# A windowed-attention block on one core: VectorE adds bias and residual in all eight tiles instead of six

## The reference

```python
xn = _ln2d(x, norm1_g, norm1_b)
xn = jnp.roll(xn, shift=(-SHIFT, -SHIFT), axis=(2, 3))
windows = _window_partition(xn, win)
attn_out = _mha(windows, in_w, in_b, out_w, out_b)
attn_out = attn_out @ proj_w.T + proj_b
y = _window_reverse(attn_out, win, hp, wp, b)
y = jnp.roll(y, shift=(SHIFT, SHIFT), axis=(2, 3))
y = shortcut + y                                # the step that the change is about
z = _ln2d(y, norm2_g, norm2_b)
z = jnp.einsum('bchw,oc->bohw', z, fc1_w) + fc1_b[None, :, None, None]
z = jax.nn.gelu(z, approximate=False)
z = jnp.einsum('bchw,oc->bohw', z, fc2_w) + fc2_b[None, :, None, None]
return y + z
```

## Time and profile before

| what | value |
|---|---|
| median of 3 runs | 91.69 us (91.31 to 93.89) |
| profiled execution, its own time | 91.67 us |
| its span, first to last instruction | 89.9 us |
| mean granted TensorE clock | 0.979 of full |
| PE busy | 80.4 us (89%) |
| DVE busy | 65.1 us (72%) |
| POOL busy | 53.3 us (59%) |
| ACT busy | 50.8 us (56%) |

### The profile page before, as it was taken

The page is one execution under the profiler, slowest core; times in us unless marked ns, Lnnn a source line. Parts: engine busy times, 40 slices in busy tenths (PEclk is TensorE's granted clock), DMA queues, the critical chain, the costliest instruction groups (busy, mean ns, idle before and its releaser), DMA issues.

```text
span 89.9 us, 4248 instructions
## 1 busy us (share of the span) xinstructions
PE 80.4 (89%) x1770; PEld 47.4 (53%) x1770; DVE 65.1 (72%) x208; ACT 50.8 (56%) x85; POOL 53.3 (59%) x64
## 2 busy tenths in 40 slices
PE   5987999888999998999997958949999999999960
PEld 5975756545774666647645525525464444243420
DVE  4999989989899799799788895992470763333060
ACT  0494998980579287485763615623449496353500
POOL 7978829982866917996954878579305225800000
PEclk9999999999999999999999999998599999999999
DMA  1899300110111111111021110000000000030233
GB/s 28 217 368 423 157 22 7 55 63 32 44 37 44 51 47 37 65 40 55 30 66 37 51 50 30 0 7 0 7 0 7 0 0 0 7 117 24 93 138 99
DMA packets 3619, 5.74 MB, mean 64 GB/s; under 512 B 1072, under 2 KB 1840, under 8 KB 3472
## 3 DMA queue, kind: packets, MB, share of 16 engines
q1 hardware_dynamic: 2736, 3.08, 10.3%
q10 hardware_dynamic: 864, 2.39, 7.1%
HBM read 2.65 MB, written 1.05 MB: 41 GB/s over the span
## 4 chain that ended last, share of the span: by engine, by line
PE 49%; POOL 19%; DVE 16%; issue 11%; ACT 1%; POOLq 0%; DVEq 0%
POOL max_x L1045 9%; PE ps_s L320 7%; PE ps_u L484 5%; PE ps_u L411 4%; PE ps_s L468 4%; POOL rstd L1054 3%; DVE stats L624 3%; PE ps_t L468 3%; POOL rstd_x L1061 3%; PE ps_t L320 3%; DVE row_max L644 3%; PE ps_m L468 2%; PE ps_o L437 2%; PE ps_o L425 2%; PE ps_o L484 2%
## 5 line engine op out<-in xcount | busy, mean ns | idle before, releaser
L1045 POOL TENSOR_TENSOR max_x<-max_t,early 128x512 bf16<-128x512 bf16 x14 | 14.7, 1049 | 11.3 <-DVE max_t L657 11.3
L644 DVE TENSOR_REDUCE row_max<-ps_s 128x16 f32<-128x1024 f32 x15 | 18.2, 1213 | 2.7 <-PE ps_s L320 2.4
L914 ACT ACTIVATE probs<-ps_t 128x1024 f32<-128x1024 f32 x13 | 13.3, 1025 | 10.2 <-PE ps_t L394 9.8
L320 PE MATMUL ps_s<-masked,qk 32*64 32x256 f32 x240 | 16.4, 386 | 1.9 <-DMA masked<-qk 0.8
L320 PE MATMUL ps_t<-masked,qk 32*64 32x256 f32 x224 | 15.3, 387 | 0.0
L1054 POOL TENSOR_TENSOR rstd<-y_var,minus_half 128x4 f32<-128x4 f32 x8 | 8.3, 1034 | 8.8 <-DVE y_var L703 8.7
L320 PEld LDWEIGHTS ps_s<-masked,qk 32*64 32x64 f32 x240 | 8.2, 131 | 5.6 <-DVE row_max L644 1.8
L411 PE MATMUL ps_u<-probs,vz 128*32 128x64 f32 x512 | 10.9, 228 | 0.0
L411 PEld LDWEIGHTS ps_u<-probs,vz 128*32 128x32 f32 x512 | 8.2, 113 | 3.6 <-issue 3.2
L1030 POOL TENSOR_TENSOR rstd<-var,minus_half 128x4 f32<-128x4 f32 x8 | 8.5, 1060 | 1.0 <-DVE var L632 0.4
L663 DVE STREAM_TRANSPOSE sums<-ps_u 128x512 f32<-128x512 f32 x8 | 5.7, 707 | 4.0 <-PE ps_u L411 4.0
(11 more groups left out here) (115 smaller groups left out, 154.9 us busy)
## 6 DMA issues: line engine op xcount, KB each, us to landing
masked<-qk SPq DMA_DIRECT2D x54, 32.0 KB, 1.9
x_ch<-x_ch_d ACTq DMA_DIRECT2D x1, 1024.0 KB, 8.3
out_d<-result SPq DMA_DIRECT2D x3, 256.0 KB, 2.5
x_tok<-x_tok_d ACTq DMA_DIRECT2D x1, 512.0 KB, 6.3
late<-late_d ACTq DMA_DIRECT2D x1, 352.0 KB, 4.6
x_tok<-x_tok_d SPq DMA_DIRECT2D x2, 128.0 KB, 3.4
x_tok<-x_tok_d ACTq DMA_DIRECT2D x1, 256.0 KB, 4.3
out_d<-result SPq DMA_DIRECT2D x2, 128.0 KB, 2.3
```

Of the source, the lines that this page charges most:

```text
L320: return nc.tensor.matmul(ps[o:o + L, g, n * TOK:(n + 1) * TOK], qk[r:r + RG, b, w, t], masked[r:r + RG, b, :, w, t], start=(n == 0), stop ...
L644: nc.vector.tensor_reduce(row_max[:, w, 0:16], score_bank(k, w)[:].rearrange("q g (h j) -> q (g h) j", j=L), axis=AX.X, op=ALU.max).then_i ...
L914: nc.scalar.activation(probs[:, w, :], scores_t_bank(k, w)[:].rearrange("q g c -> q (g c)"), ACT.Exp).then_inc(probs_done, 1)
L1045: nc.gpsimd.tensor_tensor(max_x[:, k % 2, w, :].rearrange("q (n i) -> q n i", n=16), bf16_high(max_t[:, w, :]).unsqueeze(1).to_broadcast([ ...
```

## The change

The set `SPLIT` is emptied, and what served it is taken out: the tile `y_part`, its semaphore, `bias_y` on ACT and `residual` on POOL. DVE's `residual` is called for all eight tiles.

```diff
-        y_part = sb("y_part", [P, TOK])
...
-        SPLIT = (TILES - 5, TILES - 4)
...
-                if tile_ok(t - 2) and t - 2 not in SPLIT:
+                if tile_ok(t - 2):
                     residual(t - 2)
...
-            def bias_y(k):
-                act.wait_ge(out_projected, k + 1)
-                if k > SPLIT[0]:
-                    act.wait_ge(y_done, k)
-                nc.scalar.activation(y_part[:], ps_o[:, 0, 0:TOK], ACT.Identity, bias=b_out[:, 0:1]).then_inc(y_part_done, 1)
...
-                if t - 2 in SPLIT:
-                    bias_y(t - 2)
...
-            def residual(k):
-                pool.wait_ge(y_part_done, k - SPLIT[0] + 1)
-                nc.gpsimd.tensor_tensor(y_all[:, tokens(k)], y_part[:], x_ch[:, tokens(k)], op=ALU.add).then_inc(y_done, 1)
...
-                if t - 2 in SPLIT:
-                    residual(t - 2)
```

More of the change, by code:

```diff
@@ L186, in swin_block_kernel @@
         out_projected = sem("out_projected")
-        y_part_done = sem("y_part_done")
         y_done = sem("y_done")
```

## The result

The changed kernel took 89.06 us (median of 4 runs, 88.68 to 89.17) against 91.62 us for the kernel before (4 runs, 91.31 to 93.89). The ratio is 0.9725, with a 95% interval of 0.9681 to 0.9768: 2.75% faster. The profiled execution took 89.03 us with a span of 87.2 us. The prediction said 88.0 us in a range of 87.4 to 90.4, so the direction and the range held and the point was 1.1 us low.

A forecast was written before the change was run, and what follows sets the result against it. The prediction took PE as the bound, waiting in two places for a square behind POOL's late residual. From 91.67 us it took 2.24 for the waits and 1.48 for the clock, giving 88.0 us, range 87.4 to 90.4.

The forecast's parts named there:

- What bounds the kernel: PE, busy 89%, idles 1.23 and 1.19 us before the sums of tiles 3 and 4; POOL's residual queued behind `max_x`.
- The residual costs DVE 0.40 us: DVE's added instruction per slot costs 0.40 us from start to start, read from slot 4.
- Slot 5, gain 0.87: PE's wait for the square goes; scores of slot 6 then wait for DVE's `find_max`, gaining 0.87 of 1.23 us.
- the mark for a wrong step: If PE's scores of slot 6 start later than 54.2, the step on `find_max` was wrong; 53.8 was expected.
- Slot 6, gain 1.37: PE's second wait goes with 0.18 us to spare; sums start at 58.48 instead of 60.72, 2.24 us in all.
- PE's row of steps moves as one piece, if DVE and ACT keep up: In slot 6, PE's steps from scores to `weigh_values` all move earlier by 0.87 us, to 53.82 and 58.01.
- The rival of a partial wait: Late `find_max` or `masked` DMA replaces part of PE's second wait; 90.3 to 90.8 us, chance 0.13.
- The clock, 1.48: The low clock from `y_spread` to `shift_scores` in slot 7 cost 1.48 us; the forecast took it to vanish.
- The bounds, nothing or all: After the change the low clock costs either nothing or again 1.48 us; nothing was taken.
- the stretch from 25 us to slot 5: PE's gapless stretch there shows no clock fall, taken as support for the clock staying full after the change.
- The sum: Whole kernel: 91.67 - 2.24 - 1.48 = 87.95, so 88.0 us; chance 0.50.
- DVE is the bound: Rival: DVE steps between `find_max` of slots 5 and 6 set the pace, adding 0.80 us; 92.5 us, chance 0.04.

The follow-up runs named there:

- sum_first_again: Kernel before, offload kept, with GpSimd's sum for tiles 3 and 4 moved ahead of max_x in its queue, second group: 88.59 us, ratio 0.9792.
- tile 3 alone: Changed kernel with DVE taking only tile 3's residual, tile 4's staying with ACT and GpSimd: 92.53 us.
- residual twice: Changed kernel with DVE computing the residual of tiles 3 and 4 twice, first into a spare tile: 89.00 us, ratio 0.9661.
- the shifted kernel: Changed kernel with three warm-up matmuls replaced by 23 tiny ones, moving PE's later instructions on by 80 places: 92.56 us.
- the filled kernel: Kernel before with ten matmuls of zeros on PE ahead of the channel sums in slots 5 and 6: 92.80 us, ratio 1.0151.

## Why the prediction came out as it did

- *What bounds the kernel*: right. The waits were due to the residual's place behind `max_x` in POOL's queue. This is shown: moving the sum ahead of `max_x` alone gave 88.64 us, ratio 0.9637.
- *The residual costs DVE 0.40 us*: 52.64 - 52.25 = 0.39. Right.
- *Slot 5, gain 0.87*: 1.13 in the first pair of profiles, 1.14 in the second (6.45 and 5.31 us). PE's scores of slot 6 began at 54.25, a little later than the 54.2 that I had set as the mark for a wrong step, because slot 5 itself began 0.69 late. Measured from slot 5's start, they come after 5.03 us, and 5.29 was forecast; what gave the 0.26 was not looked into. DVE was late next, as said: its second row maximum ended at 52.99 + 1.16 = 54.15, 0.10 us ahead of the scores, and doubling the residual moved them on.
- *Slot 6, gain 1.37*: 0.73. This is the step that failed, "PE's row of steps moves as one piece, if DVE and ACT keep up". They did keep up: DVE's residual of tile 4 ended at 57.56 + 0.47 = 58.03, ACT's square at 58.49, and PE came to the sums at 59.54. PE stalled for 0.6 us at the end of a packet of its own instructions, 57.06 to 58.73 in place of 1.05 us for its second scores. Before the change PE came to that place 1.81 us after the packet, and nothing was to be seen. The prediction put the arrival of PE's instructions at nothing, without a row for it. The rival of a partial wait was real in size and had another cause than the two that I named, though the keys' DMA did show up at 0.45 us in the profile of `sum_first_again`.
- *The clock, 1.48*: 1.49 in the first pair of profiles, and 1.50 between the two profiles of the kernel before. As the price of a low stretch in a median run it is a little high: in the table above a run of the kernel before with one stretch is 91.62 - 90.29 = 1.33 above one without, and one that falls where PE then waits less costs as little as 0.53. As a forecast of what the change returns it was too simple. Low stretches were seen at three places, from one execution to the next, and they were rarer after the change, 5 of 14 runs against 28 of 39. The bounds, nothing or all, were right for a pair of runs and not for medians, and that the first profile had a low stretch before and none after is in part luck. One reading was wrong: the stretch from 25 us to slot 5 isn't gapless. The earlier trace rows has tenths only, and the timeline of PE has waits of 0.26 us at 35.65 and 0.54 at 48.53 in it, with no fall behind them.
- *The sum*: without any low stretch on either side the gain is 90.29 - 88.57 = 1.72 us (2.08 and 1.55 in the two groups that hold both kernels), where 2.24 was forecast; 2.24 less the stall of 0.6 is 1.6. The rest of the measured 2.6, about 0.8, is by this table the clock, where 1.48 was forecast. The range held because it was wide enough for both.
- *DVE is the bound*: it fell as a price for the kernel. With 0.40 us more on DVE slot 5 was 0.4 us longer, and the kernel no slower. The rule of the Trainium skill that the prediction set against the change (page "Perfetto Trace Analysis", section "Optimizing Scalar/DVE Operations"), that offloading may make sense when DVE is saturated, isn't contradicted. Here, with DVE busy 3.08 of 3.20 us, the offload cost time in the place that it had in POOL's queue, and in a better place it was neither better nor worse than no offload.

## What to carry to other kernels

Before taking an offload back, look at what stands ahead of it in the queue that it was given to: one instruction for another tile, waiting for something else, can cost more than the work that was moved. A gain that you add up on the busiest engine ends where that engine meets its next limit, and one limit, the arrival of its own instructions, shows in a trace only once the other waits are gone. Where the clock of TensorE can fall, compare runs with the same number of low stretches, or the state of the clock is taken for an effect of the edit.

## What the runs showed of the hardware that was not expected

- PE's granted clock fell to 1.2 GHz behind idle stretches of only 1.19 and 1.55 us, while stretches of 1.23 and 1.34 us in the same kernels had no fall behind them. In two profiles (tile 3 alone, residual twice) it fell almost 3 us behind a wait of 0.75 and 0.72 us at 20 us that other profiles have without a fall. A low stretch cost 1.3 to 1.5 us, and 0.53 where PE had idle time behind it.
- PE waited for its instructions at fixed counts of its stream: 0.26 to 0.87 us of idle time, and 0.4 to 1.5 us with what is hidden in stretched rows, different from one execution to the next at the same place. In 13 traces it went past such a place no earlier than 1.19 us after the end of the instruction packet.
- 23 matmuls of two columns took 2.6 us at the start of the shifted kernel (46 records, 0.057 us each), where 16 of them in `y_sum` take 0.43 us (32 records, 0.013 each). The start was slow in general: the matmuls of zeros took 0.25 us a record there and 0.125 in the filled kernel at 53 us. That accounts for half of the difference; the rest is open.
